# Attention on one core: half of each probability tile split before it is turned, and turned by a DMA transpose

## The reference, cut to what matters

```python
q = jnp.einsum('bse,ehd->bshd', x, wq)
k = jnp.einsum('bse,ehd->bshd', x, wk)
v = jnp.einsum('bse,ehd->bshd', x, wv)
qn = rms_norm(q, q_scale)
kn = rms_norm(k, k_scale)
scores = jnp.einsum('bqhd,bkhd->bhqk', qn, kn)
attn = jax.nn.softmax(scores, axis=-1)
out = jnp.einsum('bhqk,bkhd->bqhd', attn, v)
return jnp.einsum('bqhd,hde->bqe', out, wo)
```

## Time and profile before

| | |
|---|---|
| median of 3 runs | 1143.24 us (1141.92 to 1145.26) |
| profiled execution, its own time | 1143.51 us |
| its span, first to last instruction | 1141.7 us |
| TensorE's mean granted clock | 0.952 of full speed |
| busy: PE, DVE, ACT, POOL | 1031.2, 824.4, 623.7, 579.8 us |
| matmul and weight-load instructions | 7790 each |

### The profile page before, as it was taken

The page is one execution under the profiler, slowest core; times in us unless marked ns, Lnnn a source line. Parts: engine busy times, 40 slices in busy tenths (PEclk is TensorE's granted clock), DMA queues, the critical chain, the costliest instruction groups (busy, mean ns, idle before and its releaser), DMA issues. The chain is left out here.

```text
span 1141.7 us, 21617 instructions
## 1 busy us (share of the span) xinstructions
PE 1031.2 (90%) x7790; PEld 688.7 (60%) x7790; DVE 824.4 (72%) x1461; ACT 623.7 (55%) x1225; POOL 579.8 (51%) x449
## 2 busy tenths in 40 slices
PE   5976989999999999999999999989978878979797
PEld 4455766666666666666666666548724345557434
DVE  3878257877887888788778887954589955866467
ACT  3564166666666666666666666742441025646532
POOL 3222457557765875587558754534148202621263
PEclk9965999999999999999999999989999978989899
DMA  5664023667677656775776567651102326759833
GB/s 176 114 199 143 2 56 65 64 104 81 92 73 104 77 93 77 104 80 88 77 101 81 87 65 91 80 133 43 57 37 79 106 89 211 223 169 299 285 90 93
DMA packets 196543, 122.34 MB, mean 107 GB/s; under 512 B 75044, under 2 KB 189782, under 8 KB 196182
## 3 DMA queue, kind: packets, MB, share of 16 engines
q1 hardware_dynamic: 178934, 97.74, 47.9%
q10 hardware_dynamic: 14432, 14.81, 3.9%
q0 software_dynamic: 3072, 8.39, 2.2%
HBM read 81.90 MB, written 36.37 MB: 104 GB/s over the span
## 5 line engine op out<-in xcount | busy, mean ns | idle before, releaser
L1293 DVE TENSOR_REDUCE a_nmax<-psum 128x1 f32<-128x1024 f32 x128 | 156.3, 1221 | 81.6 <-PE psum L1141 78.3
L1299 DVE SCALAR_TENSOR_TENSOR a_pT<-psum,a_pT 128x512 f16<-128x512 f32 x256 | 163.8, 682 | 18.5 <-ACT a_pT L1236 13.7
L1236 ACT ACTIVATE a_pT<-psum 128x512 f16<-128x512 f32 x256 | 139.7, 603 | 14.1 <-PE psum L1152 13.0
L1059 POOL TENSOR_TENSOR a_rnorm<-a_ss,a_power 128x8 f32<-128x8 f32 x32 | 57.6, 1800 | 171.4 <-DVE a_ss L1269 171.2
L1228 ACT ACTIVATE a_ex<-psum,a_nmax 128x1024 f32<-128x1024 f32 x128 | 142.8, 1116 | 0.3 <-DVE a_nmax L1293 0.2
L1152 PEld LDWEIGHTS psum<-ident,a_ex 128*128 128x128 f32 x1024 | 120.5, 141 | 25.1 <-issue 0.7
L1152 PE MATMUL psum<-ident,a_ex 128*128 128x128 f32 x1024 | 133.4, 273 | 0.0
L1123 PE MATMUL psum<-a_wh,xT_h 128*128 128x128 f16 (+1 forms) x512 | 115.3, 248 | 2.0 <-PEq L2738 2.0
L1124 PE MATMUL psum<-a_wl,xT_h 128*128 128x128 f16 (+1 forms) x512 | 115.3, 248 | 0.0
L1125 PE MATMUL psum<-a_wh,xT_l 128*128 128x128 f16 (+1 forms) x512 | 115.2, 248 | 0.0
L1163 PE MATMUL psum<-a_pT,a_vh 128*128 128x512 f16 x256 | 98.1, 383 | 6.4 <-DVE a_of L977 5.1
(11 more groups left out here) (397 smaller groups left out, 2531.9 us busy)
## 6 DMA issues: line engine op xcount, KB each, us to landing
split_gate_up<-a_e_wh SPq DMA_DIRECT2D x64, 128.0 KB
a_rb<-row_scales SPq DMA_DIRECT2D x32, 256.0 KB
g_e_gu<-split_gate_up SPq DMA_DIRECT2D x32, 256.0 KB, 3.9
block_outputs<-g_e_ym ACTq DMA_DIRECT2D x16, 512.0 KB, 4.5
split_rest<-a_e_wh SPq DMA_DIRECT2D x45, 128.0 KB
wf<-in_L_ffn_W_gate SPq DMA_DIRECT2D x32, 128.0 KB, 2.5
wf<-in_L_ffn_W_up SPq DMA_DIRECT2D x32, 128.0 KB, 2.5
wf<-in_L_ffn_W_down SPq DMA_DIRECT2D x32, 128.0 KB, 3.0
```

Of the source, the lines that this page charges most:

```text
L1236: act.activation(pT[g][:, 0, 4 * h:4 * h + 4, (m % 4) * P:(m % 4 + 1) * P], bank_of(r, unit).rearrange("p (k q) -> p k q", k=4), ACT.Copy, ...
L1293: dve.tensor_reduce(nmax[:, k:k + 1], score_banks(m), AX.X, ALU.max, negate=True).then_inc(max_ready, 1)
L1299: dve.scalar_tensor_tensor(low, bank_of(r, unit).rearrange("p (k q) -> p k q", k=4), PROB, high, ALU.mult, ALU.subtract).then_inc(low_done, 1)
```

## The change

The upper half of each tile's keys (512 of 1024) no longer goes through TensorE. While still queries by keys, it is split where it lies: ScalarE writes its high part (`half_high`) and VectorE its low part (`half_low`) from `ex` into one of four buffers, which lie in the room of `x` (`halves`). SP then turns high and low of a tile by one DMA transpose of 128 x 1024 float16 (`turn_half`) straight into `pT`. The lower half goes as before. So `tile` has no halves any more: four transposes, one ScalarE and one VectorE instruction from PSUM, and beside them one of each from `ex`. `values` waits for the turned halves ahead of its third piece, and `half_high` for the transpose that read its buffer four tiles ago. As `x` is overwritten, the tokens are loaded again behind the attention (`load_tokens`). SP's order is written anew around the eight transposes of a head, and the split weights are stored with fewer, larger runs.

```diff
@@ -828,14 +836,13 @@
             two = slice(4 * t + 2 * j, 4 * t + 2 * j + 2)
+            sp.dma_start(self.gu[two, :, :, :].rearrange("e p a x -> p e (a x)"),
+                         self.blocks[b][:, 0:2, :, :].rearrange("p e a x -> p e (a x)")).then_inc(self.stored[b], 16)
+            sp.dma_start(self.dn[two, :, :, :].rearrange("e f a d -> (e f) (a d)"),
+                         self.blocks[b][:, 2, :, :].rearrange("p a d -> p (a d)")).then_inc(self.stored[b], 16)
+        else:
             for part in range(2):
-                sp.dma_start(self.gu[two, :, part, :].rearrange("e p x -> p e x"),
-                             self.halves[b][:, part, 0:2 * self.GU].rearrange("p (e x) -> p e x", e=2)).then_inc(self.stored[b], 16)
-            sp.dma_start(self.dn[two, :, :, :].rearrange("e f a d -> (e f) a d"), self.halves[b][:, :, 2 * self.GU:])\
-              .then_inc(self.stored[b], 16)
-        else:
-            for at in range(0, self.WIDTH, D):
-                sp.dma_start(self.rest[:, :, t * self.WIDTH + at:t * self.WIDTH + at + D], self.halves[b][:, :, at:at + D])\
+                sp.dma_start(self.rest[:, part, t * self.WIDTH:(t + 1) * self.WIDTH], self.parts[b][:, part, :])\
                   .then_inc(self.stored[b], 16)
...
@@ -859,6 +866,8 @@
     VB = 3
+    BY_DMA = NT // 2
+    SPLIT = 4
     QT = NT
...
@@ -933,13 +942,17 @@
         ex = [tmp(f"ex{b}", [P, T]) for b in range(2)]
-        pT = [tmp(f"pT{b}", [P, 2, KT, HALF], F16) for b in range(2)]
+        pT = [tmp(f"pT{b}", [P, KT, 2, HALF], F16) for b in range(2)]
+        room = env["x"][:, :, :].rearrange("p n d -> p (n d)").bitcast(F16)
+        halves = [room[:, b * 2 * HALF:(b + 1) * 2 * HALF].rearrange("p (k a q) -> p k a q", a=2, q=P) for b in range(SPLIT)]
         rb = [tmp(f"rb{g}", [P, HALF]) for g in range(2)]
...
         wo_loaded = sem("a0_wol")
+        p_high, p_low = sem("a0_ph"), sem("a0_pl")
+        p_turned = [sem(f"a0_pt{b}") for b in range(SPLIT)]
         row_stored, row_loaded = ([sem(f"a0_{n}{g}") for g in range(2)] for n in ("rst", "rld"))
...
@@ -957,6 +970,26 @@
             return [("side", ahead, s) for s in sides] if coming(t, ahead) else []
+        def half_of(m):
+            return slice((NT - BY_DMA) * P, None), halves[m % SPLIT], pT[m // 4], slice((m % 4) * P, (m % 4 + 1) * P)
+        def wait_half_free(engine, t, m):
+            if QT * t + m >= SPLIT:
+                engine.wait_ge(p_turned[m % SPLIT], 16 * ((QT * t + m) // SPLIT))
+        def turn_half(sp, t, m):
+            _, half, out, cols = half_of(m)
+            sp.wait_ge(p_low, QT * t + m + 1)
+            if m % 4 == 0 and t > 0:
+                sp.wait_ge(pv_ready, 2 * t + m // 4 - 1)
+            sp.dma_start_transpose(out[:, NT - BY_DMA:, :, cols].rearrange("p k a q -> p (k a) q"),
+                                   half.rearrange("p k a q -> p (k a q)")).then_inc(p_turned[m % SPLIT], 16)
+        def wait_turned(engine, t, g):
+            for m in range(4 * g, 4 * g + 4):
+                engine.wait_ge(p_turned[m % SPLIT], 16 * ((QT * t + m) // SPLIT + 1))
...
@@ -994,7 +1027,16 @@
-        env["last_half"] = (last_scales, split_stored, last_high, last_low, o_low, 2 * H)
+        def load_tokens(sp):
+            for g in range(2):
+                wait_turned(sp, H - 1, g)
+            tokens = w["L0_attn_x"][0].rearrange("(n p) d -> p n d", p=P)
+            for i, loaded in enumerate(env["x_loaded"]):
+                tiles = slice(i * X_TILES, (i + 1) * X_TILES)
+                sp.dma_start(env["x"][:, tiles, :], tokens[:, tiles, :]).then_inc(loaded, 16)
+        env["last_half"] = (last_scales, split_stored, last_high, last_low, o_low, 2 * H, load_tokens)
         with nc.Block() as block:
...
@@ -1012,30 +1054,47 @@
                     experts.load(sp, k)
+                def next_chunk(k):
+                    experts.store(sp, k)
+                    if k == 3 * (H - 2) + 1:
+                        experts.wait_stored(sp, 18)
+                    if k + 2 < 3 * H:
+                        experts.load(sp, k + 2)
                 for t in range(H):
+                    last = t == H - 1
+                    turn_half(sp, t, 0)
                     if t + 3 < H:
                         load(t + 3)
+                    for m in range(1, 4):
+                        turn_half(sp, t, m)
                     store_scales(t, 0)
-                    if t == H - 1:
+                    if last:
                         load_scales(sp, t, 0)
...
                         sp.wait_ge(made, unit_count(H - 2, ("side", 1, NS - 1)))
-                        for part, dst in enumerate(env["wo_halves"]):
-                            sp.dma_start(dst.rearrange("p h e -> p (h e)"), env["split_rest"][:, part, 0:H * D])\
-                              .then_inc(wo_loaded, 16)
-                    for j in range(3):
-                        if j == 1 and t < H - 1:
-                            load_scales(sp, t, 0)
-                        if j == 2:
-                            store_scales(t, 1)
-                        experts.store(sp, 3 * t + j)
-                        if t == H - 2 and j == 1:
-                            experts.wait_stored(sp, 18)
-                        if 3 * t + j + 2 < 3 * H:
-                            experts.load(sp, 3 * t + j + 2)
-                    if t < H - 1:
+                    else:
+                        next_chunk(3 * t)
+                    for m in range(4, QT):
+                        turn_half(sp, t, m)
+                        if last:
+                            part, heads_at = (m - 4) // 2, slice((m % 2) * H * D // 2, (m % 2 + 1) * H * D // 2)
+                            sp.dma_start(env["wo_halves"][part].rearrange("p h e -> p (h e)")[:, heads_at],
+                                         env["split_rest"][:, part, heads_at]).then_inc(wo_loaded, 16)
+                        else:
+                            if m == 4:
+                                load_scales(sp, t, 0)
+                            if m == 5:
+                                next_chunk(3 * t + 1)
+                            if m == 6:
+                                next_chunk(3 * t + 2)
+                    store_scales(t, 1)
+                    if last:
+                        for j in range(3):
+                            next_chunk(3 * t + j)
+                    else:
                         load_scales(sp, t, 1)
-                sp.wait_ge(wo_loaded, 32)
+                sp.wait_ge(wo_loaded, 64)
...
@@ -1141,25 +1200,26 @@
-                def tile(t, m, h, r):
-                    unit = ("tile", m, h)
-                    if h == 0:
-                        pe.wait_ge(exp_ready, QT * t + m + 1)
+                def tile(t, m, r):
+                    unit = ("tile", m)
+                    pe.wait_ge(exp_ready, QT * t + m + 1)
                     wait_bank(t, unit)
                     out = bank_of(r, unit)
-                    for k in range(4):
-                        last = pe.transpose(out[:, k * P:(k + 1) * P], ex[m % 2][:, (4 * h + k) * P:(4 * h + k + 1) * P], ident[:, :])
+                    for k in range(NT - BY_DMA):
+                        last = pe.transpose(out[:, k * P:(k + 1) * P], ex[m % 2][:, k * P:(k + 1) * P], ident[:, :])
                     last.then_inc(made, 1)
...
                     if piece == 0:
-                        pe.wait_ge(low_done, low_count(t, ("tile", 4 * g + 3, 1)))
+                        pe.wait_ge(low_done, low_count(t, ("tile", 4 * g + 3)))
                         if not (fixed(t) and t == 0 and g == 0):
                             pe.wait_ge(of_ready, 2 * t + g)
+                    if piece == 2:
+                        wait_turned(pe, t, g)
                     out, vh, vl = psum[:, O_BANK, :], v_h[r % VB], v_l[r % VB]
                     for k in (2 * piece, 2 * piece + 1):
-                        ph, pl = (pT[g][:, part, k, :] for part in range(2))
+                        ph, pl = (pT[g][:, k, part, :] for part in range(2))
                         pe.matmul(out, vh[:, k, :], ph, start=(k == 0), stop=False)
...
@@ -1222,19 +1281,28 @@
-                        act.wait_ge(made, unit_count(t, ("tile", m - 2, 1)) if m >= 2 else unit_count(t - 1, ("tile", QT + m - 2, 1)))
+                        act.wait_ge(made, unit_count(t, ("tile", m - 2)) if m >= 2 else unit_count(t - 1, ("tile", QT + m - 2)))
+                        act.wait_ge(p_low, QT * t + m - 1)
                     if k == 0 and not (fixed(t) and t == 0):
...
-                def tile(t, m, h, r):
-                    unit, g = ("tile", m, h), m // 4
+                def tile(t, m, r):
+                    unit, g = ("tile", m), m // 4
                     act.wait_ge(made, unit_count(t, unit))
-                    if m % 4 == 0 and h == 0 and not (fixed(t) and t == 0):
+                    if m % 4 == 0 and not (fixed(t) and t == 0):
```

(32 more changed lines are left out.)

38 lines of the change are left out of this document (27 added, 11 removed).

## The result

| | before | after |
|---|---|---|
| median | 1144.25 us (1141.92 to 1145.93, 4 runs) | 1232.99 us (1231.47 to 1235.07, 4 runs) |
| span of the profiled execution | 1141.7 us | 1232.1 us |
| TensorE's mean granted clock | 0.952 | 0.913 |

A forecast was written before the change was run, and what follows sets the result against it. SP's DMA queue was to bound the attention at 42.9 us a head: 15 periods less 3 x 1.42 give 639.2 us for 566.6, +72.6; with +1 for the ends, 1217 us from 1143.5, range 1140 to 1265.

The forecast's parts named there:

- ScalarE's waits for a buffer: Attention: ScalarE's high part waits for the transpose reading its buffer, so SP's lateness reaches TensorE, some 8 us a head.
- TensorE's saving: Attention: half its transposes go, 56 us in all, 3.5 us a head, leaving 34.7 us a head for TensorE alone.
- The queue's chain: SP's DMAs from one head's first reciprocals' store to the next's: 40.9 us, 42.9 with drains.
- chunk 1: Third term of SP's sum: store and reload of a weight chunk, 4.15 us with two store DMAs for three.
- The drain of 0.4 us at five places: SP's queue: extra hold of an ordinary DMA following a transpose, 0.4 us each (0 to 0.8), five places a head.
- the last term: End of SP's sum: next head's tile 0 transpose 1.25, projection weights 1.42, three transposes 3.75 us.
- The price of a transpose: SP's queue: each DMA transpose holds it 1.25 us (1.19 to 1.6), a cost taken to go with size.
- These cost nothing while SP is slower: ScalarE and VectorE work in a head: VectorE at worst 4 us more, 34.3 us, hidden under slower TensorE or SP.
- What I had as one bound: Next below SP's queue in a head: TensorE alone, at 34.7 us.
- the queue theory: Attention: SP's serial queue with two bare landings sets the head, so a covered landing gives its time back.
- The row with 26 GB/s: Profile row: DMA rate behind a reciprocals' store, used to add 0.5 us for tile 4's transpose to the first landing.
- The ends: First head's start, last head's tail and the tokens' second load, outside the 15 head periods: together +1 us.

The follow-up runs named there:

- Experiment 9: The changed kernel with each DMA transpose cut to the first two of its four key blocks: 1219.84 us, ratio 1.0635.
- experiment 6: The changed kernel with GpSimd's passes over the second layer's weight chunks cut to a few columns: 1231.41 us, ratio 1.0753.
- the first two experiments: Experiments 1 and 2, changed kernel: second reciprocals' load moved behind the next head's first four transposes, 1227.34 us; first load also moved behind chunk 1, 1231.26 us.
- experiment 4: The changed kernel with reciprocals stored as 128 runs of 16 bytes instead of 512 single numbers, scaling not the reference's: 1170.50 us, ratio 1.0163.
- experiment 7: The changed kernel with reciprocals stored as 16-byte runs, plus GpSimd's passes over the second layer's chunks cut to a few columns: 1148.89 us, ratio 1.0038.
- experiment 8: The kernel before with GpSimd's passes over the second layer's chunks cut to a few columns: 1138.32 us, ratio 0.9948.
- experiment 5: The changed kernel with the second reciprocals' load behind the second of the next head's first four transposes: 1201.19 us, ratio 1.0502.
- experiment 12: The changed kernel with the 4-byte stores issued by ScalarE's queue and the row loads moved later in SP's: 1227.28 us, ratio 1.0735.

## Why the prediction was right, and where it was off

The direction, the cause and the range held: 1217 us forecast, 1233 measured, 1140 to 1265 given. The path from SP to TensorE held too: ScalarE's waits for a buffer were forecast as some 8 us once a head, and are 86.1 us in 15.5 heads, 5.6 each.

*TensorE's saving* is there (512 transposes of probabilities for 1024) and worth nothing, as said: SP's queue set the head. It is also smaller than the 56 us forecast. TensorE's busy time fell by 10.9 us only (1031.2 to 1020.3), and its mean granted clock from 0.952 to 0.913. It stood idle for 5.19 us up to 443.96, at the start of the head shown, and in the 10 us from 443.10 on it was granted 0.75 on average, which is half of the time at the lower of its two levels, 1.2 GHz. The prediction's 34.7 us for TensorE alone took the full clock for granted.

*The queue's chain.* Forecast and measured for the head of 443.06, by the numbers of the sum: to the load that waits, 11.3 and 11.54; the load and tile 5, 1.68 and 1.88; chunk 1, 4.15 and 4.99; tile 6, 1.25 and 1.31; chunk 2 and tile 7, 5.60 and 5.65; the second landing and its load, 10.48 and 10.05; tile 0, the weights and three transposes, 6.42 and 7.36. The sum was 40.9 without drains, 42.9 with them, and is 42.78.

*The drain of 0.4 us at five places was wrong.* An ordinary DMA behind a transpose takes 0.53 to 0.65 us where it took 0.33 to 0.47, so 0.1 to 0.3 each, about 1 us in all for 2.0 forecast. The other microsecond came from elsewhere: chunk 1 was 0.8 us dearer, of which 0.1 is such a drain, and the three transposes of the last term took 1.3 to 1.5 us each. That 42.9 met 42.78 is partly luck.

*The price of a transpose* was right, 1.25 for a median of 1.31, by a wrong reason. I scaled it by the number of blocks. Experiment 9 shows a price that hardly depends on size.

*"These cost nothing while SP is slower"* held for VectorE's growth: with it partly undone, 4.2 us of the stretch came back (experiment 6, whose ratio can't be told from the changed kernel's). But the size was missed: 5.1 us a head, where 4 was "at worst", nearly all of it by one cause that I hadn't read out of L982's maximum of 1176 ns. The instructions of GpSimd beside those long ones would have shown it.

*The average head* took 43.3 us for 42.6 (the 15 first periods 649.8 us for 639.2). Those 10.6 us are the larger part of what the forecast missed; the head above is among the shorter ones, and where the others lose more wasn't followed up.

*What I had as one bound were two.* My text has TensorE at 34.7 right below the queue, and the first two experiments' expectations, 1120 to 1140, were made from that. With short landings the head stays at 610.1 / 15.5 = 39.4 us, and VectorE is why in part (experiments 4 and 6 to 8).

*The landing as something that only SP waits for* was the wrong part of the queue theory. During these 10 us other transfers crawl, whether the small writes came by SP's queue or by ScalarE's, and what is issued in that time is soon held itself. So a landing was covered at best in part by DMA work, which is what experiments 1, 2, 5 and 12 tried. The row with 26 GB/s said so, and I used it for 0.5 us only.

*The ends* were +1 and came out at +7.2 (90.4 less the 83.2 of the 15 periods): the tokens' load waits behind the last landing, and the first addition to x waits for it:

```profile
868.15 0.54 DVE L2252 TENSOR_TENSOR x<-x,g_gated 128x256 f32<-128x256 f32 x1 [7.74 <-DMA x<-in_L_attn_x]
```

7.74 us for the 3 (0 to 4) given.

## What to carry to other kernels

Before work moves from an engine to DMA, look at what the DMA engines do in the stretch, not only at their mean share: two stores of 512 numbers of 4 bytes each took some 20 of a head's 43 us to land; stored as runs of 16 bytes, the bare landing took 2.2. A latency that is free today is free by the work that stands under it in the queue; write down which, and see whether the change takes it away. And when an operand moves from PSUM to on-chip memory, look at which instructions of VectorE then have two such operands, and what GpSimd runs beside them. And before a row of waits is believed, look in the timeline whether the waiting engine has a gap there.

## What the runs showed of the hardware

- Behind a store of 512 single 4-byte numbers the load that waits for its landing goes out 8.5 to 10.2 us later, with nothing in between (the changed kernel's second stores); behind one of 128 runs of 16 bytes, 2.2 us. While the first kind lands and other DMAs are queued, 32 to 97 GB/s move in all, for 191 (experiment 12, 451.00 to 458.70) and 215 (changed kernel, 456 to 467) in stretches of chunks and transposes without it.
- A DMA transpose within on-chip memory holds the queue 1.24 us for 128 x 1024 elements and 1.19 for 128 x 512, when nothing holds it longer.
- Some 4 us behind such a store, with seven DMAs issued since, the next transpose is held for 5 to 7 us in most heads; with half-size transposes three of 16 are held for 7.7 to 7.9, and one that stands right behind the store isn't. A hold of 8.66 us is seen too where the store came by ScalarE's queue. Lack of room in SP's queue would explain all of it and wasn't measured by itself.
- VectorE's split with both operands on chip takes 0.68 us with GpSimd idle and up to 2.37 us beside GpSimd; with one operand in PSUM, 0.66 to 0.69 always. VectorE's multiply with a row read at a step of 16 bytes takes 1056 ns for 681.
